# Attention kernel: the loop over batches written out, and VectorE's evictions moved behind each step's first maximum

## What is computed

```python
x = _layernorm(x + _L0_attn_ref(x, Wqkv, Wout))
x = _layernorm(x + _L0_xattn_ref(x, ctx, ctx, w_q, b_q, w_k, b_k, w_v, b_v, w_o, b_o))
x = _layernorm(x + _L0_ffn_ref(x, gate_w, we_gate, we_up, we_down, ws_gate, ws_up, ws_down))
```

## Time and profile before

| | |
|---|---|
| median of three runs | 1383.52 us (1378.53 to 1386.51) |
| the profiled execution's own time | 1384.98 us |
| its span in the profile | 1383.2 us |
| first scores of S0 to last exponential of C7 | 55.1 to 999.4 us |
| C0 (`second`, written out) and C1 (`second`, in the loop) | 58.9 and 58.7 us |
| S3, S4, S5, S6 (`first`, in the loop) and S7 (`first`, written out) | 61.4, 61.4, 61.4, 63.0 and 60.6 us |
| granted TensorE clock, mean | 0.979 of 2.4 GHz |
| stretches at 1.2 GHz within attention | 5, near 163, 221, 344, 706 and 883 us |

### The profile page before, as it was taken

The page is one execution under the profiler, slowest core; times in us unless marked ns, Lnnn a source line. Parts: engine busy times, 40 slices in busy tenths (PEclk is TensorE's granted clock), DMA queues, the critical chain, the costliest instruction groups (busy, mean ns, idle before and its releaser), DMA issues. The chain is left out here.

```text
span 1383.2 us, 27264 instructions
## 1 busy us (share of the span) xinstructions
PE 1306.8 (94%) x8312; PEld 774.9 (56%) x8312; DVE 1078.5 (78%) x2227; ACT 923.6 (67%) x1776; POOL 454.1 (33%) x487
## 2 busy tenths in 40 slices
PE   3999999999999999999999999999988999999996
PEld 2534444444444444444444444443466799999985
DVE  5889888888988987897888888889668755555557
ACT  3387777677777777777777777768736655565555
POOL 3334203401510240151024020102136636666663
PEclk9699999999999999999999999999999999999998
DMA  5453434344424433442443344234045466767695
GB/s 170 131 169 130 125 130 120 121 130 130 139 71 139 127 111 127 127 144 65 138 127 113 125 134 137 66 110 131 17 154 188 148 215 121 152 138 163 114 188 164
DMA packets 110089, 181.47 MB, mean 131 GB/s; under 512 B 20368, under 2 KB 67600, under 8 KB 105872
## 3 DMA queue, kind: packets, MB, share of 16 engines
q1 hardware_dynamic: 90576, 155.70, 35.6%
q0 software_dynamic: 18816, 23.60, 9.8%
q10 hardware_dynamic: 576, 0.79, 0.3%
HBM read 99.67 MB, written 79.30 MB: 129 GB/s over the span
## 5 line engine op out<-in xcount | busy, mean ns | idle before, releaser
L808 ACT ACTIVATE prob<-ps_sc 128x512 f32<-128x512 f32 x1024 | 551.1, 601 | 194.1 <-PE ps_sc L1070 193.4
L851 DVE TENSOR_REDUCE nm<-ps_ring 128x1 f32<-128x512 f32 x1024 | 638.5, 679 | 52.0 <-PE ps_ring L1055 51.5
L1055 PE MATMUL ps_ring<-qk 48*128 48x512 f32 x1024 | 407.4, 471 | 12.1 <-DMA qk<-hbm_self 7.4
L1070 PE MATMUL ps_sc<-qk 50*128 50x512 f32 x1024 | 388.5, 453 | 10.9 <-ACT prob L808 10.0
L1070 PEld LDWEIGHTS ps_sc<-qk 50*128 50x128 f32 x1024 | 161.2, 186 | 302.6 <-ACT prob L808 217.0
L1087 PE MATMUL ps_out<-prob,va 128*32 128x512 f32 x2048 | 276.9, 613 | 1.6 <-ACT ot L678 0.7
L1933 PE MATMUL ps_gu<-x2f,we 128*128 128x256 f32 (+1 forms) x1320 | 214.4, 317 | 1.0 <-ACT sg L1576 0.4
L1933 PEld LDWEIGHTS ps_gu<-x2f,we 128*128 128x128 f32 x1320 | 183.5, 191 | 15.0 <-ACT sg L1576 1.5
L1055 PEld LDWEIGHTS ps_ring<-qk 48*128 48x128 f32 x1024 | 166.8, 189 | 42.3 <-DVE nm L851 26.2
L607 POOL TENSOR_TENSOR rstd<-mv,eps 128x2 f32<-128x2 f32 x32 | 6.2, 195 | 345.3 <-DVE mv L939 345.3
L1933 PE MATMUL ps_dn<-we,hf 128*128 128x256 f32 x864 | 115.5, 285 | 2.9 <-DVE hf L1792 2.9
(11 more groups left out here) (185 smaller groups left out, 1595.2 us busy)
## 6 DMA issues: line engine op xcount, KB each, us to landing
qk<-hbm_cross SPq DMA_DIRECT2D x384, 64.0 KB, 2.3
qk<-hbm_self SPq DMA_DIRECT2D x372, 64.0 KB, 2.3
hbm_self<-stage SPq DMA_DIRECT2D x16, 1024.0 KB, 3.8
hbm_cross<-stage SPq DMA_DIRECT2D x16, 1024.0 KB, 4.1
slots_x<-zeros SPq DMA_DIRECT2D x8, 1360.0 KB, 5.9
xs<-slots_x SPq DMA_DIRECT2D x40, 272.0 KB, 4.0
weraw<-w_moe SPq DMA_DIRECT2D x11, 768.0 KB, 4.6
xin<-x SPq DMA_DIRECT2D x9, 512.0 KB, 4.3
```

The lines of the kernel that those rows point to most:

```text
L808: nc.scalar.activation(prob[:, s % 2, j, :], ps_sc[:, score_bank(h.cur, HG * s + j), :], ACT.Exp, scale=HD ** -0.5).then_inc(exp_done[a], 1)
L851: nc.vector.tensor_reduce(nm[:, g % 2, r:r + 1], bank(slot), axis=AX.X, op=ALU.max, negate=True).then_inc(max_done[a], 1)
L1055: nc.tensor.matmul(bank(slot), qk[rows, 0, pair, P * c:P * c + P], qk[rows, 1, pair, :], start=True, stop=True).then_inc(smax_done[a], 1)
L1070: nc.tensor.matmul(ps_sc[:, score_bank(inst, n), :], qk[rows, 1, h // 2, P * c:P * c + P], qk[rows, 0, h // 2, :], start=True, stop=True). ...
```

## The change

The loop of `every_period` becomes a plain Python loop, so that all engines get four turns written out, with constants in place of registers. VectorE's `half` reads out, ahead of m0, only what is not in `AFTER_FIRST` (v and cv, for which it has nothing to do); the read-outs of all other jobs come between m0 and m1. Steps without maxima stay as they were, and so do `nm`, TensorE, ScalarE and the jobs' order.

```diff
+AFTER_FIRST = ("ck", "cq", "xt", "nt0", "nt1", "q", "k", "w0", "w1", "ot0", "ot1")
@@ every_period
-            with eng.Fori(3, B - 1) as k:
+            for k in range(3, B - 1):
                 half(first(k, second(k - 1)))
                 half(second(k, first(k)))
@@ block.vector, half
-                    for kind, n, b, of in h.behind(s):
-                        if kind not in ("nm0", "nm1"):
+                    behind = h.behind(s)
+                    for kind, n, b, of in behind:
+                        if kind not in ("nm0", "nm1") and not (turn and kind in AFTER_FIRST):
                             task(kind, n, b, of.get((kind, n)))
                     for j in range(HG):
+                        if j == 1 and turn:
+                            for kind, n, b, of in behind:
+                                if kind in AFTER_FIRST:
+                                    task(kind, n, b, of.get((kind, n)))
                         if j == NM_AT + 1:
```

## The result

The changed kernel takes 1411.27 us (median of four runs, 1407.36 to 1412.12) against 1383.42 us: 27.9 us slower, ratio 1.0197, 95% interval 1.0177 to 1.0218. The forecast was 1408, with a range of 1387 to 1431. The profiled execution is the fastest of the four (1407.36 us, span 1405.6). Its span lies 22.4 us above that of before, less than the 27.9 us between the medians; its granted clock is 0.984, that of the other three 0.979 to 0.981, that of the profile before 0.979.

What follows compares the result with a forecast made beforehand. Attention was taken as a chain of three engines coupled by four banks. Losses of 17.1 + 1.5 + 10.4 less the loop's 4.4 gave +24.6 us on the 1383.5 median, 1408.1, said as 1408; range 1387 to 1431.

Steps and rivals of the forecast that it cites:

- C2, s5 and s8: Light steps of a `second` half: VectorE's lag partly taken up in s5, 0.25 us, and s8 gains 0.27 us.
- C2, s9 and s10: `second` half: w's later read-out costs the job waiting for m1 0.34 us; the v job gives 0.33 back.
- The read-out that lies while VectorE waits for m0: Finished q, k, ot blocks lie until m0 is reduced, delaying TensorE's m3; 1.18 us each in `second` halves' s3 and s4.
- nm at ot's bank: s5 of `first` halves: nm waits for ot's later-freed bank, with all TensorE's queue behind it; 1.25 us lost.
- The gains at ScalarE's kinds: Where VectorE waits for ScalarE (ck, cq, xt), a maximum fills the wait; 0.9 us gained per `first` half.
- the 0.15 taken off for s7: `first` half's sum of 1.45 us taken as 1.3, since a later TensorE leaves ScalarE less behind in s7.
- The 0.62 us for ot: VectorE's time to read ot, placed from 1.16 to 1.78 us after TensorE's m0 in the step timings.
- The loop: Writing out four turns removes three ways back in S4, S5 and S6, 1.45 us each; 4.4 us gained.
- That longer code costs nothing: Fetching the written-out loop's longer code was taken as 0, as already written-out halves show no such stall.
- 17.1 + 1.5 + 10.4: Move's loss in us: six halves like `second` 17.1, S0 1.5, eight halves like `first` 10.4.
- the third rival: TensorE's 1.2 us stands cause one more clock fall in every half from S1 on; 24 us more, 1432; chance 0.15.
- The other two rivals: VectorE drifts behind, filling waits: 1365 or 1372, chance 0.09; or light steps take up losses: 1384 to 1389, chance 0.13.

Runs made afterwards that it cites:

- the loop alone: Kernel before with only the loop written out, VectorE's order unchanged; ratio 0.9996 against the kernel before.
- q and k alone: Loop written out, only q and k read behind the first maximum, all else ahead of it as in the kernel before; ratio 1.0101 against that kernel.
- the doubled dose: Loop written out, only q and k held back, but behind the second maximum instead of the first; ratio 1.0236 against the kernel before.
- the one ot put back ahead: Changed kernel, except that the fourth ot of a half is read ahead of the first maximum again; ratio 1.0161 against the kernel before.
- ScalarE's kinds alone: Loop written out, only ck, cq, nt and xt read behind the first maximum, the rest ahead of it; ratio 0.9897 against the kernel before.
- xt alone: Loop written out, only xt read behind the first maximum; ratio 0.9921 against the kernel before.
- the move alone: Changed kernel with the loop put back, so only VectorE's order differs from the kernel before; ratio 1.0270 against that kernel.

## Why the prediction was right, step by step

Lengths of steps in us, from the starts of TensorE's scores 0. The reference for S4 is the run with the loop alone, since in before its s0 holds the way back.

| | forecast | measured |
|---|---|---|
| C2, s0 and s1 | +0.57, +0.43 | +0.64, +0.44 |
| C2, s3 and s4 | +1.18, +1.18 | +1.29, +1.27 |
| C2, s5 and s8 | -0.25, -0.27 | -0.27, -0.20 |
| C2, s9 and s10 | +0.34, -0.33 | +0.25, -0.32 |
| C2, whole half | +2.85 | +3.10 |
| S4, s3 and s4 | +0.45 each | +0.53, +0.53 |
| S4, s5 | +1.25 | +1.26 |
| S4, s15 | +0.2 | 0.0 |
| S4, gains in s0 to s2, s9 to s12, s13 and s14 | -0.9 | -0.12, -0.31, -0.45 |
| S4, whole half | +1.3 | +1.43 |
| ways back, each (changed kernel against before) | -1.45 | -1.40, -1.35, -1.48 |

- *The read-out that lies while VectorE waits for m0* is shown, by the timeline of the changed kernel, by q and k alone (0.62 a step) and by the doubled dose (0.60 more for one maximum more).
- *nm at ot's bank* is shown: the one ot put back ahead returned 1.25 us in each of eight halves, 9.9 in all.
- *The gains at ScalarE's kinds* are shown by the run with them alone. Their term was right in size; that it would be outweighed was the forecast. The items of a `first` half added up to 1.45 and came out at 1.43; the 0.15 taken off for s7 did not show, s7 is as long as before. The 0.62 us for ot is not what the earlier trace rows show (0.73, since q's product waits there for its block); in the changed kernel it is 0.63, so the times from m0 hold.
- *The loop.* 4.2 us over three ways back, 4.4 forecast; this holds the 0.06 us that the move adds to each s0, and with the loop alone it is 4.4. That longer code costs nothing was nearly right: one step of S6 is 0.3 us longer.
- *Mis-sized: the halves that are not the pattern.* S2 and C5 lose in s9 (5.17 us against 4.86) and s11 (3.30 against 3.05), where S3 to S6 gain in s9 and s10; they cost 2.3 each instead of 1.3. C0 to C4 cost 3.1 instead of 2.85, S1 about as much. S0 cost 3.4 instead of 1.5: q or k lies behind the maximum in four of its steps, and the clock takes part of it (below). In all, with the clock's falls from S1 on taken out, the move costs 34.5 us, where the forecast had 29.0 (17.1 + 1.5 + 10.4).
- *Left at nothing: the clock.* The forecast's sum has no term for it, and the third rival, which has one, put one more fall in every half. The sign was the other: the five falls of before, which cost 1.55 us each in S1, S3 and S6 and 0.83 in S2 and C5 (6.3 in all, read as the difference of s13 or s14 to a half of the same kind without a fall), are all absent from both profiles of the changed kernel. Only in S0 did the rival hold. TensorE is recorded busy 2.31 of the 3.40 us from 54.0 on, at full clock, and then has half of it until 60.9 us (granted 0.51); before, the clock is full from 56.7 on. s0 of S0 is 5.59 instead of 3.73 us; 0.64 is the usual loss of such a step, and the 1.2 that remain fit the clock.
- *The sum.* 34.5 - 4.4 - 6.3 - 1.4 (the parts ahead of S0 and behind C7) = 22.4 us, the difference of the two spans. The 34.5 is what the other terms leave, so this sum has to close; the changes of the single halves add up to the same. The forecast of 24.6 lies between these 22.4 and the 27.9 between the medians. So 1408 for a measured 1411.27 rests partly on two errors of opposite sign, 5.5 us too little for the order and 6.3 us of clock not counted. That the other three executions took 3 to 5 us more at a lower granted clock fits falls that the profiled one did not have; their traces weren't read, so this stays open.
- The other two rivals did not come true: VectorE does not drift behind TensorE in s3 to s5, it waits 1.24 us there. Of the loss, s5 takes up the 0.27 us that the forecast had counted, and s6 and s7 nothing; the 0.20 of s8 is there with ScalarE's kinds alone too, so it isn't loss taken up.

What brings the falls is open. All those between S1 and C7 but one begin in s13 or s14, the steps around xt. With xt read behind a maximum there were 0, 0, 0, 0, 0, 0, 1 and 1 of them between S1 and C7 in eight profiles (the second 1 in the run with xt alone, the first at a way back of the loop), with xt read ahead 5, 2, 1 and 1 in four. That points to the stand in s13, and the one in the run with xt alone shows that it isn't the whole cause. The length of an idle stretch doesn't tell it either: in the 14 us ahead of the falls of before, TensorE's longest recorded idle time is 0.40 to 0.91 us, while the changed kernel has one of 1.2 us in s5 of each of eight halves and no fall behind any. So the third rival's reason, that stands of 1.2 us bring falls, has no support here.

## What to carry to other kernels

A consumer that reads buffers in another order than the producer makes them pays twice: it stands until the later one is made, and the producer then stands at the earlier one's buffer. Holding a read-out back pays only where it waits for a third engine, and only as much as its wait; so move by kind, and look up for each buffer who takes it next and what is queued behind that user. Work that frees no buffer (here w's moments) is better placed behind all that does; that gained 9.6 us.

## What the runs showed of the hardware

- A program's way back in a loop cost ScalarE 2.2 us of idle time ahead of its first instruction; written out, it is 0.3 to 0.8. VectorE waits for ScalarE there in the kernel before (2.73 us at 412.07); in the run with the move alone, where it needn't, it stood 2.57 and 2.24 us for its own issue in S5 and S6. TensorE, which jumped in the same turn, started its scores without a gap (529.86 us).
- TensorE's granted clock fell to 1.2 GHz for 3.4 us at a time where its longest recorded idle time in the 14 us before was 0.40 to 0.91 us (kernel before), at a cost of 0.8 to 1.6 us each; behind eight idle stretches of 1.2 us in the changed kernel it didn't fall. From S1 on there were 5 falls before, 2 with the loop alone written out, and none in both profiles of the changed kernel.
- The same part behind attention took 383 to 384 us in four of the profiles and 401 to 409 in the eight taken on the first two chips of the experiments, while halves of attention with the same code agreed to 0.1 us.
